# Decay sums of a chunked state-space layer: from a matmul per chunk to differences of spread running sums

## The reference

```
dA     = dt * A                          # [token, head]
A_cum  = cumsum(dA) inside a chunk
L      = exp(segsum(dA))                 # L[l, s] = exp(A_cum[l] - A_cum[s]) for s <= l, else 0
Y_diag = einsum(C, B, L, x * dt)         # inside a chunk
states = einsum(B, exp(A_cum[-1] - A_cum), x * dt)
Y_off  = C @ state carried from the chunks before, times exp(A_cum)
y      = Y_diag + Y_off + D * x;  y = rmsnorm(y * silu(z));  h1 = res + y @ out_proj_w
```

## Time and profile before

| | us |
|---|---|
| median of 3 runs | 827.72 (825.9 to 828.43) |
| the profiled execution | 825.34 |
| its span, first to last instruction | 823.5 |
| PE busy | 729.5 (89%) |
| DVE busy | 586.4 (71%) |
| POOL busy | 307.6 (37%) |
| ACT busy | 227.1 (28%) |
| prologue of sequence 0 | 0 to 44.3 |
| chunk parts of sequences 0 to 3 begin at | 44.3, 138.8, 231.7, 323.0 |
| MLP and projection parts begin at | 83.1, 175.2, 268.2, 366.6 |
| experts | from 433 on |

### The profile page before, as it was taken

How to read it: one execution, slowest core, us unless ns; L and a number is a source line. 1 busy time by engine, 2 the same in 40 slices (tenths; PEclk the granted TensorE clock), 3 DMA queues, 4 the chain that set the end, 5 groups by cost and what they waited for, 6 DMA issues and landing times.

```text
span 823.5 us, 10260 instructions
## 1 busy us (share of the span) xinstructions
PE 729.5 (89%) x2718; PEld 463.9 (56%) x2719; DVE 586.4 (71%) x1385; ACT 227.1 (28%) x481; POOL 307.6 (37%) x505
## 2 busy tenths in 40 slices
PE   2987999889998999969807999999999999999972
PEld 1455547664566547644603666666666666666642
DVE  3777845878477865843543888888888888888880
ACT  1473434635444534631102111111111111111110
POOL 2147202732447215631342343344333443344322
PEclk9999999999999999978858999999999999999995
DMA  9700000000010000038726221111211121111111
GB/s 315 289 2 1 0 1 26 27 1 0 2 51 0 0 0 26 27 112 290 110 80 236 77 32 32 26 25 29 35 25 25 25 32 32 25 25 30 27 13 13
DMA packets 30166, 43.72 MB, mean 53 GB/s; under 512 B 4099, under 2 KB 23875, under 8 KB 30128
## 3 DMA queue, kind: packets, MB, share of 16 engines
q1 hardware_dynamic: 21600, 33.15, 12.6%
q0 software_dynamic: 8544, 10.30, 7.7%
HBM read 33.84 MB, written 9.75 MB: 53 GB/s over the span
## 4 chain that ended last, share of the span: by engine, by line
PE 66%; DVE 10%; issue 9%; POOL 9%; DMA 2%; ACT 2%; DVEq 0%; SPq 0%; POOLq 0%; ACTq 0%
PE ps L688 28%; PE ps L697 14%; PE ps L390 5%; PE ps L401 3%; PE ps L357 3%; PE ps L546 3%; PE ps L551 3%; POOL lists L1397 2%; POOL big L1375 2%; DVE big L1294 2%; PE ps L475 1%; PE ps L565 1%; PE ps L373 1%; DVE big L1002 1%; POOL big L1370 1%
## 5 line engine op out<-in xcount | busy, mean ns | idle before, releaser
L1294 DVE STREAM_TRANSPOSE big<-big 32x224 f32<-32x224 f32 x624 | 251.2, 403 | 9.3
L688 PE MATMUL ps<-big 128*128 x624 | 242.7, 542 | 1.1 <-ACT big L910 1.1
L688 PEld LDWEIGHTS ps<-big 128*128 128x128 f32 x624 | 119.1, 191 | 106.0 <-issue 104.1
L1332 POOL TENSOR_TENSOR big<-big 128x1 f32<-128x1 f32 x179 | 56.6, 316 | 279.8 <-DVE big L1302 180.8
L697 PE MATMUL ps<-big 128*128 x546 | 126.9, 385 | 6.3 <-DVE big L1302 5.6
L697 PEld LDWEIGHTS ps<-big 128*128 128x128 f32 x546 | 102.5, 193 | 20.1 <-issue 7.3
L357 PE MATMUL ps<-big 128*128 128x128 f32 (+1 forms) x320 | 53.4, 290 | 57.8 <-DMA big<-lists,big 15.6
L916 ACT ACTIVATE big<-ps 128x896 f32<-128x896 f32 x39 | 35.8, 917 | 217.1 <-PE ps L688 217.1
L357 PEld LDWEIGHTS ps<-big 128*128 128x128 f32 (+1 forms) x320 | 40.7, 150 | 86.6 <-issue 43.6
L1309 DVE TENSOR_TENSOR big<-big,ps 128x896 f32<-128x896 f32 x39 | 42.4, 1088 | 47.5 <-PE ps L688 47.3
L1473 POOL DMA_INDIRECT out_rows<-big x39 | 63.3, 1623 | 23.5 <-issue 23.5
(11 more groups left out here) (169 smaller groups left out, 933.8 us busy)
## 6 DMA issues: line engine op xcount, KB each, us to landing
big<-in_w SPq DMA_DIRECT2D x24, 896.0 KB, 8.6
out_rows<-big SPq DMA_DIRECT2D x4, 512.0 KB, 2.9
xn_rows<-big SPq DMA_DIRECT2D x4, 512.0 KB, 4.1
big<-in_hidden SPq DMA_DIRECT2D x1, 1536.0 KB, 13.9
big<-in_in_proj SPq DMA_DIRECT2D x1, 1288.0 KB, 8.7
big<-in_gate SPq DMA_DIRECT2D x1, 640.0 KB, 13.2
big<-in_up SPq DMA_DIRECT2D x1, 640.0 KB, 7.1
big<-in_down SPq DMA_DIRECT2D x1, 640.0 KB, 7.4
```

The source lines that it names most:

```text
L688: last = mm(bank(bk + n)[:, 0:HALF], xT[:, k, :], expert_cols(e, off + k * M + n * HALF, HALF), start=(k == 0), stop=(k == KD - 1))
L1294: last = V.transpose(hTs[c * SQ:(c + 1) * SQ, half, :].rearrange("p (j t) -> p j t", j=MB)[:, :, q * SQ:(q + 1) * SQ], ha[q * SQ:(q + 1) * ...
L1332: G.tensor_tensor(idle[:, k:k + 1], half[:, 0:1], half[:, 0:1], ALU.add)
```

## The change

The exponents `A_cum[l] - A_cum[s]` are no longer a matmul. `dec_` gets a fourth small matmul, which gives the running sums of all chunks and heads as 32 rows of 128. ScalarE copies these (`cumT`) and the same sums by token (`cums`). SP writes the rows to DRAM (`cum_rows`) and reads them back, in one transfer per chunk, into all 128 partitions of `em` (`spread`; each partition gets the same 4 KB). GpSimd subtracts the sum of its own token and clamps to at most 0 (`apart`, two instructions on 128 x 1024 per chunk), and ScalarE takes the exponential in place. `em` has four buffers, `mda` is gone. All four chunks are done ahead: `spread(b + 1)` is the first thing in SP's body, `apart` of the four chunks stands on GpSimd behind the scale of h2 and in front of the scatter, and `decay` of the four chunks on ScalarE behind the MLP's last gate, that of chunk 0 before the copies of `front`, the others behind them. `seg_` is gone from TensorE, with its waits. `decayed_x` moves from VectorE to GpSimd, behind `scaled_x` of the same chunk. `yT_` writes to bank 5 in place of bank 0, and the wait for `h1_` of the chunk before moves from it to `out_`. In the prologue SP waits for the sums of sequence 0 before it issues the loads of the first two experts.

```diff
+    cum_rows = nc.dram_tensor("cum_rows", [CH * HEADS, P], F32).ap()
...
-        mda = cols(2, HEADS * P)
-        em = cols(2, HEADS * P)
+        em = cols(CH, HEADS * P)
...
+        cums = cols(CH, HEADS)
+        cumT = cols(P)
...
+            def spread(n):
+                sp.wait_ge(cumT_taken, nth(n, 1, 0))
+                if not (isinstance(n, int) and n == 0):
+                    sp.wait_ge(y_ps, n * CH)
+                sp.dma_start(cum_rows, cumT[0:CH * HEADS, :]).then_inc(cum_out, 16)
+                sp.wait_ge(cum_out, nth(n, 16, 15))
+                for c in range(CH):
+                    sp.dma_start(em[:, c, :].unsqueeze(1),
+                                 cum_rows[c * HEADS:(c + 1) * HEADS, :].rearrange("(o h) l -> o (h l)", o=1).unsqueeze(0).to_broadcast([P, 1, HEADS * P])).then_inc(cum_in[c], 16)
+            spread(0)
...
+                if nxt:
+                    spread(b + 1)
...
-                last.then_inc(dec_ps, 1)
+                mm(bank(1)[0:CH * HEADS, P:2 * P], dA.rearrange("p a b -> p (a b)"), tri_upto, start=True, stop=True).then_inc(dec_ps, 1)
...
-            def seg_(b, c, prev):
-                pe.wait_ge(mda_ready, nth(b, CH, c))
-                if c > 0:
-                    pe.wait_ge(seg_taken, nth(b, CH, c - 1))
-                else:
-                    pe.wait_ge(conv_taken, nth(b, CB, CB - 1))
-                for i in range(2):
-                    last = mm(bank(4 + i), tri_after, mda[:, c % 2, i * 512:(i + 1) * 512], start=True, stop=True)
-                last.then_inc(seg_ps, 1)
...
-                    last = mm(bank(6)[:, hh * HD:(hh + 1) * HD], em[:, c % 2, hh * P:(hh + 1) * P],
+                    last = mm(bank(6)[:, hh * HD:(hh + 1) * HD], em[:, c, hh * P:(hh + 1) * P],
...
             def yT_(b, c):
                 pe.wait_ge(y4_ready, nth(b, CH, c))
+                for j in range(4):
+                    last = transposed(bank(5)[:, j * P:(j + 1) * P], yb[:, c % 2, j * P:(j + 1) * P])
+                last.then_inc(yT_ps, 1)
+            def out_(b, c):
+                pe.wait_ge(yT_taken, nth(b, CH, c))
                 if c > 0:
                     pe.wait_ge(o_taken, nth(b, CH, c - 1))
-                for j in range(4):
-                    last = transposed(bank(0)[:, j * P:(j + 1) * P], yb[:, c % 2, j * P:(j + 1) * P])
-                last.then_inc(yT_ps, 1)
...
-            seg_(0, 0, False)
...
-                    if c + 1 < CH:
-                        seg_(b, c + 1, prev)
...
-                    if nxt and j == JB - 2:
-                        seg_(b + 1, 0, True)
...
+                A(cumT[0:CH * HEADS, :], bank(1)[0:CH * HEADS, P:2 * P], ACT.Copy).then_inc(cumT_taken, 1)
+                A(cums.rearrange("p a b -> p (a b)"), bank(1)[:, CH * HEADS:2 * CH * HEADS], ACT.Copy).then_inc(cums_taken, 1)
...
-                act.wait_ge(seg_ps, nth(b, CH, c))
-                A(em[:, c % 2, :], bank(4, 2), ACT.Exp).then_inc(seg_taken, 1)
+                act.wait_ge(apart_ready, nth(b, CH, c))
+                A(em[:, c, :], em[:, c, :], ACT.Exp).then_inc(decays, 1)
...
-                A(yTs.rearrange("p a b -> p (a b)"), bank(0), ACT.Copy).then_inc(yT_taken, 1)
+                A(yTs.rearrange("p a b -> p (a b)"), bank(5), ACT.Copy).then_inc(yT_taken, 1)
...
             decay(0, 0)
             front(0, 0)
+            for c in range(1, CH):
+                decay(0, c)
             def body(b, prev, nxt):
                 x_D(b, 0)
                 for c in range(CH):
                     if c + 1 < CH:
-                        decay(b, c + 1)
                         front(b, c + 1)
...
                     A(sg[dst, j % 2, :], bank(2 * (j % 2) if j < JB - 1 else 7)[src, :], ACT.Silu).then_inc(gate_taken, 1)
-                    if nxt and j == JB - 2:
-                        decay(b + 1, 0)
-                if nxt:
+                if nxt:
+                    decay(b + 1, 0)
                     front(b + 1, 0)
+                    for c in range(1, CH):
+                        decay(b + 1, c)
...
-                v.wait_ge(seg_taken, nth(b, CH, c))
-                V.tensor_tensor(heads(em[:, c % 2, :]), heads(em[:, c % 2, :]),
+                v.wait_ge(decays, nth(b, CH, c))
+                V.tensor_tensor(heads(em[:, c, :]), heads(em[:, c, :]),
...
-            def decayed_x(b, c):
-                v.wait_ge(xdt_ready, nth(b, CH, c))
-                if c == 0:
-                    v.wait_ge(dec_taken, nth(b, 1, 0))
-                V.tensor_tensor(heads(xdtd[:, c % 2, :]), heads(xdt[:, c % 2, :]), over_head(dec[:, 0, c, :]), ALU.mult).then_inc(xdtd_ready, 1)
...
-            decayed_x(0, 0)
...
-                    if c + 1 < CH - 1:
-                        decayed_x(b, c + 1)
...
-                        if t == 1:
-                            decayed_x(b + 1, 0)
...
-            def masked_dA(n, c):
-                g.wait_ge(dA_ready, nth(n, 1, 0))
-                if not (isinstance(n, int) and n == 0 and c < 2):
-                    g.wait_ge(seg_ps, n * CH + c - 1)
-                G.tensor_tensor(heads(mda[:, c % 2, :]), tri_upto.unsqueeze(1).to_broadcast([P, HEADS, P]),
-                                over_head(dA[:, c, :], P), ALU.mult).then_inc(mda_ready, 1)
+            def apart(n, c):
+                g.wait_ge(cums_taken, nth(n, 1, 0))
+                g.wait_ge(cum_in[c], nth(n, 16, 15))
+                G.tensor_tensor(heads(em[:, c, :]), heads(em[:, c, :]), over_head(cums[:, c, :], P), ALU.subtract).then_inc(apart_step, 1)
+                g.wait_ge(apart_step, nth(n, CH, c))
+                if not isinstance(n, int):
+                    pass_wait(8)
+                G.tensor_scalar(em[:, c, :], em[:, c, :], 0.0, None, ALU.min).then_inc(apart_ready, 1)
             def scaled_x(b, c):
                 g.wait_ge(xs_taken, nth(b, CH, c))
                 G.tensor_tensor(heads(xdt[:, c % 2, :]), heads(xs), over_head(dtv[:, c, :]), ALU.mult).then_inc(xdt_ready, 1)
+            def decayed_x(b, c):
+                g.wait_ge(xdt_ready, nth(b, CH, c))
+                if c == 0:
+                    g.wait_ge(dec_taken, nth(b, 1, 0))
+                G.tensor_tensor(heads(xdtd[:, c % 2, :]), heads(xdt[:, c % 2, :]), over_head(dec[:, 0, c, :]), ALU.mult).then_inc(xdtd_ready, 1)
             def plus_x_D(b, c):
                 g.wait_ge(xsd_ready, nth(b, CH, c))
@@ -1404,17 +1408,17 @@
             for k in range(4):
...
-            masked_dA(0, 0)
-            masked_dA(0, 1)
+            for c in range(CH):
+                apart(0, c)
             scaled_x(0, 0)
+            decayed_x(0, 0)
             def body(b, prev, nxt):
                 for c in range(CH):
-                    if c + 2 < CH:
-                        masked_dA(b, c + 2)
                     if c + 1 < CH:
                         scaled_x(b, c + 1)
+                    if c + 1 < CH - 1:
+                        decayed_x(b, c + 1)
                     if c > 0:
                         plus_x_D(b, c)
                         scale_y(b, c - 1)
@@ -1430,12 +1434,13 @@
...
                 if nxt:
-                    masked_dA(b + 1, 0)
-                    masked_dA(b + 1, 1)
+                    for c in range(CH):
+                        apart(b + 1, c)
                 if prev:
                     scatter(b - 1)
                 if nxt:
                     scaled_x(b + 1, 0)
+                    decayed_x(b + 1, 0)
                 for n, ts in ([(b, ALL)] if nxt else HALVES):
```

More of the change, by code:

```diff
@@ L248, in build @@
         z_ps, z_taken = map(sem, ("z_ps", "z_taken"))
-        xs_ps, xs_taken, bg_ps, bg_taken, seg_ps, seg_taken = map(sem, ("xs_ps", "xs_taken", "bg_ps", "bg_taken", "seg_ps", "seg_taken"))
-        mda_ready, xdt_ready, xdtd_ready, xsd_ready, em_ready = map(sem, ("mda_ready", "xdt_ready", "xdtd_ready", "xsd_ready", "em_ready"))
+        xs_ps, xs_taken, bg_ps, bg_taken = map(sem, ("xs_ps", "xs_taken", "bg_ps", "bg_taken"))
+        cumT_taken, cums_taken, cum_out, apart_step, apart_ready, decays = map(sem, ("cumT_taken", "cums_taken", "cum_out", "apart_step", "apart_ready", "decays"))
+        cum_in = tuple(map(sem, ("cum0_in", "cum1_in", "cum2_in", "cum3_in")))
+        xdt_ready, xdtd_ready, xsd_ready, em_ready = map(sem, ("xdt_ready", "xdtd_ready", "xsd_ready", "em_ready"))
         off_ps, off_scaled, y_ps, y_taken, s_ps, s_taken, y3_ready, y4_ready, ssy_ready, ry_ready = map(sem, ("off_ps", "off_scaled", "y_ps", "y_taken", "s_ps", "s_taken", "y3_ready", "y4_ready", "ssy_ready", "ry_ready"))
@@ L471, in out_ @@
                 pe.wait_ge(yT_taken, nth(b, CH, c))
+                if c > 0:
+                    pe.wait_ge(o_taken, nth(b, CH, c - 1))
                 if isinstance(b, int) and b == 0 and c == 0:
@@ L1326, in _ @@
             G = nc.gpsimd
-            idle = cols(8)
+            idle = cols(9)
             def pass_wait(k):
```

4 lines of the change are left out of this document (removed).

## The result

| | before | after |
|---|---|---|
| median of 20 runs, us | 826.35 (823.19 to 828.43) | 830.89 (824.92 to 839.33, and one of 1526.74) |
| profiled execution, us | 825.34 | 837.67 |
| its span, us | 823.5 | 835.9 |
| mean granted clock | 0.956 | 0.922 |

The changed kernel is slower: ratio 1.0045, 95% interval 1.0023 to 1.0067, some 3.7 us. The forecast was 819. The ratio leaves out six slow runs of the changed kernel, the one of 1526.74 us and five of 837.4 to 839.3, the profiled one among them; with those five the means differ by 0.7%. The profiled execution of after lies 6.8 us above its median, so its stages show where time was lost but overstate how much: the span grew by 12.4 us, the median by 4.5.

A forecast was written before the change was run, and what follows sets the result against it. TensorE bounds the MLP part, a chain between TensorE, VectorE and GpSimd the chunk parts. -4.3 - 4.8 - 4.0 + 0.3 + 3.0 + 1.5 = -8.3 us, 825.34 to 817.0 profiled, 819 median; 8-in-10 range 811 to 830.

The forecast's parts named there:

- Step 5: MLP part: `apart`, clamp at 1.5 us, overlaps routing in sequences 1 and 2; +3.0 us, bounds 0 and +10.
- Step 4: Prologue, sequence 0: new chain to `apart`, done by 48 to 50; +0.3 us, bounds -1 and +4.
- Step 6: TensorE's clock: one more fall from 2.4 to 1.2 GHz; +1.5 us, bounds -3.4 and +7.
- Step 1: MLP part: `seg_` leaves full TensorE in sequences 0 to 2 (-5.2), added `dec_` matmul costs +0.9; sum -4.3 us.
- Step 2: Chunk parts, sequences 1 and 2: shorter VectorE queue, own yT bank; -2.4 us each, -4.8 for two; bounds 0 and -4.
- Rival D: Chunk parts: VectorE's time was free, GpSimd with decayed x becomes the bound; -1.8 us in all, 826; chance 0.10.
- Step 3: Sequence 3's chunks, set by VectorE and TensorE, get shorter; -4.0 us, bounds -1 and -6.
- A: Clamp holds VectorE through all of route_pick in the MLP parts; 10 us in place of 3, 826; chance 0.13.
- B: Spread reads from DRAM are slow, from about 7 us a transfer, delaying prologue and MLP; 836 median; chance 0.09.
- C: TensorE's clock falls in every chunk part and one more behind it; +7 in place of 1.5, 825; chance 0.06.

The follow-up runs named there:

- e8_all: Changed kernel with clamp and decayed x on VectorE, first next-sequence decay before the last gate, prologue's x times D before decays 1 to 3; 815.97 us, ratio 0.9868.
- e10_act_order: Changed kernel with only ScalarE's order altered: first next-sequence decay before the last gate, prologue's x times D before decays 1 to 3; 828.89 us, ratio 1.0019.
- e4_dec_dve: Changed kernel with decayed x back on VectorE, all else as changed; 825.97 us, ratio 0.9992.
- e7_clamp_dve: Changed kernel with the clamp moved from GpSimd to VectorE, GpSimd only subtracting; 823.24 us, ratio 0.9956.
- e12_all_bank0: e8_all with yT in bank 0 again; 819.41 us, ratio 0.9905.
- e6_keep: Changed kernel plus two unused 512-column matmuls at each of the three former places of `seg_` in a chunk part; 829.45 us, ratio 1.0029.
- e9_all_keep: e8_all plus two unused 512-column matmuls at each former place of `seg_` in a chunk part; 816.37 us, ratio 0.9879.

## Why the prediction was wrong

The forecast was -8.3 us; +3.7 came. The step that failed is 5, the price of `apart`: its clamp was put at 1.5 us and took 2.77. Step 4 takes that price over and failed with it. Step 6, one more fall of the clock, was too small as well.

- **Step 1, seg_ out of the MLP part (-4.3 in three parts): holds.** The added matmul took 0.34 us for two instructions. The gain shows once the wait is gone and parts with the same clock are compared: 53.7 (e8_all, M1) against 55.0 (before, M2) at 1.00, and 55.4 (e8_all, M2) against 56.7 (before, M1) at 0.97, so -1.3 each time. In the change M0 grew by 2.0 instead: on ScalarE the first decay of the next sequence stands behind the last gate, and TensorE waits 1.36 us in the down projection. The forecast had put that order at nothing; e10_act_order takes 1.4 us of it back.
- **Step 2, chunk parts (-2.4 each): the size holds (-2.8, -1.8), the reason doesn't.** I put 1.3 to 1.4 of it on decayed x; with decayed x on VectorE the parts are as short (33.5, 33.8), and the move alone brings nothing (1.0001). Rival D was right on this point. What is left to explain the gain is the masked multiply that left GpSimd: in e4_dec_dve xn_ is 1.26 us shorter than in the earlier trace rows, where I counted 0.8, and L1032 (L1026 of before) starts 12.5 us after the end of the last down-matmul (248.03 less 235.53), where before it was 14.6 (246.48 less 231.91). No run has the masked multiply's removal alone. The gain isn't safe either: with a clock of 0.86 the part is 36.5 us (e7_clamp_dve). The own bank, 0.3 a part in the forecast, is nearer 3 us for the whole kernel. How it gets there isn't settled: in e12_all_bank0 C1 is 2.0 us longer than in e8_all, and its rows show a clock fall in that stretch, which may be its effect or chance.
- **Step 3, sequence 3 (-4.0): holds** (-3.5).
- **Step 4, the prologue (+0.3, bounds -1 and +4): +4.9.** The chain up to the first `apart` was right (35 forecast, 34.83 measured). Four clamps, each 1.27 us longer than forecast, made its end 54.2 and not 48 to 50. The forecast looked at x times D on ScalarE; what TensorE waits for is scaled x, behind the last clamp on GpSimd, and putting x times D first changes nothing (e10_act_order). With the clamp off GpSimd P+C0 is 65.9. The clock, 1.00 before, is 0.85 here and 0.87 in e7_clamp_dve.
- **Step 5, `apart` under the routing (+3.0, bounds 0 and +10).** The clamp was mis-sized: 1.5 forecast, at most 1.89, 2.77 measured. I had bounded a one-input operation from above by the two-input one of its size, as if an input less could not cost more. In sequence 2 `apart` ends 35.5 us after `dt` (311.7 less 276.18), where the forecast had 29.4 (297.5 less 268.15), and lies across all of the routing (first operation 28.2 us after `dt`). The waits are 2.4 and 2.6 us, and behind them the clock's fall costs 2.9 and 2.8: 10.7 us in the profiled execution, just over my upper bound. Of the 2.6 us the subtraction beside L1096 makes 1.6 and the clamp beside L1098 0.8: the clamp's length did its harm mostly by pushing the last subtraction into the routing. The clamp taken off GpSimd gives 7.4 us in the ratios, prologue included.
- **Step 6, clock (+1.5, bounds -3.4 and +7): too small.** I counted one more fall at 1.7 us. The table has a lower clock in all seven stages, and a fall behind a wait costs 2.8 to 2.9. Parts M1 and M2 of the versions without `seg_` line up by it (the two with the clamp on ScalarE aside): without the wait for `positions` 53.7 us at 1.00 and 55.4 to 55.6 at 0.97; with it 56.2 and 56.5 at 1.00 (e4_dec_dve, e6_keep), 58.1 at 0.97, 59.9 at 0.94, 60.9 to 61.3 at 0.92, 62.9 at 0.89. So the wait alone costs what it lasts, and the growth of M1 by 6.2 us is -1.3 (`seg_`), +2.4 (wait) and some +5 (clock), that of M2 the same: an estimate from these rows. What lowers it is in part the missing matmuls (e6_keep, e9_all_keep), but putting them back gives no gain clear of noise, so what this is worth stays open.
- **Rivals.** A was the mechanism, with 0.13: its price (10 us in place of 3) is what M1 and M2 show. What it left out is that the same clamp also makes the prologue late, which puts the total on the slow side and not at 826. B is refuted: the 16 spreads land in 3.9 to 7.5 us (median 5.5, not the under 4 that I had named), and what ScalarE waits for in the prologue is the last clamp. C's sign was met (0.85, 0.95 and 0.90 in the chunk parts), its cause is shown for the clock and not for the time.

The Trainium skill on this: "SBUF — State Buffer", "SBUF: two separate sides", has a VectorE operation with two SBUF inputs blocked until a GpSimd instruction that reads SBUF and started first is through. The subtraction does that (L1096 is held until it ends); beside the clamp of 304.06 the routing's two-input operations took 0.19 to 0.35 us, beside the next one L1098 took 1.01 and ended 1.7 us before the clamp did, while L1118 (two inputs, 0.84 from 310.87) and L1119 ended with it. So for the clamp the rule fits a part of the rows only, and its length hurt mostly through what it pushed late. "GPSIMD Engine Reference", "Elementwise — side-by-side cycle accounting", has 1.03 cycles per element, by which the clamp was an estimated 1.0 us; the trace has 2.77.

## What to carry to other kernels

Don't bound an operation's time on GpSimd by a "harder" one with more inputs: only a row of the same operation counts, and where there is none, leave the bound open upwards and try the operation on another engine too (here VectorE: 0.84 us against 2.77). When work is done ahead on GpSimd, ask what VectorE does beside it, and what is queued behind it; moving a VectorE operation there can hand its time back as longer neighbours. Compare stages at the same granted clock: here the same part took 33.4 or 36.5 us, and 55.4 or 53.7, by the clock. A change that has a good core can be hidden by one such operation: the same idea ended 1.8% below the kernel before once the clamp and decayed x stood on VectorE and the order on ScalarE and the place of the clamps were right.

## What the runs showed of the hardware

- GpSimd's minimum with a constant on 128x1024 (float32) takes 2.77 us, its two-input subtraction of the same size 1.90. VectorE does the minimum in 0.69 us (median of 16; two in a row in 1.29) and in 1.6 to 2.0 beside GpSimd's subtractions.
- One 4 KB piece of DRAM read into all 128 partitions lands within the range of ordinary 512 KB transfers: 4.5 us for the first, 3.9 to 7.5 with a median of 5.5 for 16 that were issued in fours; ordinary ones of that size took 3.5 and 9.9 in the kernel before.
- Behind a wait of 2.4 to 2.7 us TensorE ran at 1.2 GHz for some 6 us in the change (3.76 and 2.89 us for eight instructions of 512 columns that take 3.8 at 2.4 GHz). Behind the same wait it stayed at 2.4 GHz in e6_keep, where TensorE has 5.2 us more of matmuls in each chunk part, but also in M2 of e4_dec_dve, which has none of these.
- With those matmuls left out the mean granted clock fell from 0.948 to 0.958 (64 runs of the kernel before) to 0.920 to 0.936 (19 runs); with unused ones in their place it was 0.942 to 0.955 (12 runs), while the time did not change clear of noise.
